# Attention over one core: PSUM banks of the score ring and the logit ring shared out as four and two in place of three and three

## The reference

```python
xn = _ln(x, norm_s_w, norm_s_b)
spatial_out = _spatial_experts(xn, idx_s, sp_in_w, sp_in_b, sp_out_w, sp_out_b)
xt = _ln(x, norm_t_w, norm_t_b)
temporal_out = _temporal_experts(xt, idx_t, tq_w, tq_b, tk_w, tk_b, tv_w, tv_b, tp_w, tp_b)
fused = _cross_mha(spatial_out, temporal_out, cross_in_w, cross_in_b, cross_out_w, cross_out_b)
x = x + fused
h2 = _ln(x, norm_mlp_w, norm_mlp_b)
x = x + (jax.nn.gelu(h2 @ mlp_w1.T + mlp_b1, approximate=False) @ mlp_w2.T + mlp_b2)
```

## Time and profile before

| What | Value |
|---|---|
| Median of 3 runs | 1720.06 us (1719.16 to 1722.15) |
| Profiled execution | 1724.92 us |
| its span, first to last instruction | 1723.1 us |
| mean granted clock of TensorE | 0.937 |
| TensorE busy | 1531.3 us (89%) |
| VectorE busy | 1244.2 us (72%) |
| ScalarE busy | 1103.0 us (64%) |
| GpSimd busy | 1021.3 us (59%) |

### The profile page before, as it was taken

The page is one execution under the profiler, slowest core; times in us unless marked ns, Lnnn a source line. Parts: engine busy times, 40 slices in busy tenths (PEclk is TensorE's granted clock), DMA queues, the critical chain, the costliest instruction groups (busy, mean ns, idle before and its releaser), DMA issues. The chain is left out here.

```text
span 1723.1 us, 37357 instructions
## 1 busy us (share of the span) xinstructions
PE 1531.3 (89%) x8662; PEld 660.2 (38%) x8662; DVE 1244.2 (72%) x3454; ACT 1103.0 (64%) x2137; POOL 1021.3 (59%) x1375
## 2 busy tenths in 40 slices
PE   2767965889999999999999999999999999875998
PEld 0215962233333333333333333333333333212665
DVE  4995865578787878878787887878788787453442
ACT  1433760647877777787877778777777778824333
POOL 6841434366685676667576667658667675432443
PEclk9767976889999999999999999999999999957999
DMA  1321116355464565465465456446546544030221
GB/s 40 77 54 30 45 30 101 50 78 73 72 81 63 71 76 77 59 80 75 59 79 76 70 64 83 64 62 86 66 70 74 82 55 63 2 37 26 62 67 55
DMA packets 134645, 109.27 MB, mean 63 GB/s; under 512 B 24128, under 2 KB 127552, under 8 KB 134592
## 3 DMA queue, kind: packets, MB, share of 16 engines
q1 hardware_dynamic: 132544, 104.45, 41.1%
q0 software_dynamic: 2048, 4.20, 1.0%
HBM read 19.26 MB, written 8.39 MB: 16 GB/s over the span
## 5 line engine op out<-in xcount | busy, mean ns | idle before, releaser
L1124 ACT ACTIVATE probs<-psum 128x512 f32<-128x512 f32 (+3 forms) x1536 | 750.0, 549 | 276.3 <-PE psum L1232 269.1
L1020 DVE TENSOR_REDUCE mx_S<-psum 128x1 f32<-128x512 f32 x512 | 324.7, 679 | 54.1 <-PE psum L1212 54.1
L1020 DVE TENSOR_REDUCE mx_C<-psum 128x1 f32<-128x512 f32 x512 | 317.6, 676 | 35.7 <-PE psum L1212 35.7
L1016 DVE CUSTOM_DVE_ANT_0 psum<-psum,causal 128x128 f32<-128x128 f32 (+3 forms) x512 | 241.4, 516 | 101.5 <-PE psum L1212 100.3
L1212 PE MATMUL psum<-ks_C,qs_C 96*128 96x512 bf16 x512 | 199.8, 398 | 12.1 <-DVE mx_C L1020 9.4
L1212 PE MATMUL psum<-ks_S,qs_S 96*128 96x512 bf16 x512 | 196.9, 395 | 13.3 <-DVE mx_S L1020 9.4
L1232 PE MATMUL psum<-qs_S,ks_S 99*128 99x512 bf16 x512 | 189.0, 385 | 5.4 <-ACT probs L1124 5.4
L1232 PE MATMUL psum<-qs_C,ks_C 99*128 99x512 bf16 x512 | 188.9, 387 | 4.7 <-ACT probs L1124 4.4
L903 POOL CAST parts_q<-f_q 128x512 bf16<-128x512 f32 x48 | 29.3, 611 | 261.8 <-ACT f_q L1115 261.4
L1212 PE MATMUL psum<-ks_T,qs_T 96*128 96x128 bf16 (+3 forms) x512 | 156.7, 308 | 6.4 <-DVE mx_T L1016 4.3
L1232 PE MATMUL psum<-qs_T,ks_T 99*128 99x256 bf16 (+3 forms) x512 | 152.7, 302 | 6.2 <-ACT probs L1124 3.3
(11 more groups left out here) (182 smaller groups left out, 2722.2 us busy)
## 6 DMA issues: line engine op xcount, KB each, us to landing
qs_S<-parts_q SPq DMA_DIRECT2D x96, 128.0 KB, 4.4
ks_S<-parts_k SPq DMA_DIRECT2D x96, 128.0 KB, 5.0
qs_T<-parts_q SPq DMA_DIRECT2D x96, 128.0 KB, 4.4
ks_T<-parts_k SPq DMA_DIRECT2D x96, 128.0 KB, 4.6
qs_C<-parts_q SPq DMA_DIRECT2D x96, 128.0 KB, 4.4
ks_C<-parts_k SPq DMA_DIRECT2D x96, 128.0 KB, 4.7
w_in_S<-in_s_in SPq DMA_DIRECT2D x16, 257.0 KB, 2.7
w_in_T<-in_t_in SPq DMA_DIRECT2D x16, 257.0 KB, 2.6
```

The costliest lines, as they stand in the source:

```text
L1016: nc.vector.tensor_tensor_reduce(tile[:, 0:last_key], tile[:, 0:last_key], causal[:, T - last_key:T], 1.0, NEG, ALU.add, ALU.max, mx[kind] ...
L1020: nc.vector.tensor_reduce(mx[kind][:, n:n + 1], tile, AX_X, ALU.max, negate=True).then_inc(reduced, 1)
L1124: nc.scalar.activation(probs[:, group_place(kind, b, n // 4), n % 4, t0:T], psum[:, LOGITS + ring_place(kind, b, n, RC), t0:T], ACT.Exp, s ...
```

## The change

The score ring gets a fourth bank and the logit ring gives one up. The bank of the weighted sums (6) and the desk (7) stay where they are. Score tile n then waits for the reduction of tile n-4 in place of n-3, and logit tile n for the exponential of tile n-2 in place of n-3. The logit ring begins at bank 4 in place of 3; the fold of weights ahead of the loop, which borrows the first two logit banks, moves with it.

```diff
-RL, RC, RP = 3, 3, 3
+RL, RC, RP = 4, 2, 3
```

## The result

The changed kernel takes 1826.05 us (median of 4, 1821.69 to 1827.05) against 1720.05 (median of 4 on the same chip): 1.0612 of the time before, 95% interval 1.0599 to 1.0625. The forecast was 1810 (1738 to 1840), slower.

A forecast was written before the change was run, and what follows sets the result against it. TensorE's own work and short stalls were taken to set the loop's period; 7.1 lost less 1.1 kept gives 6.0 us a cycle, times 15 cycles 90 us, so 1810 us (1738 to 1840).

The forecast's parts named there:

- What bounds the kernel: Attention loop, cycle 76.2 us: TensorE's own work and its short stalls set the period; no other engine is full.
- Part 2, the third logit bank: Attention loop: logit tiles wait for exponential n-2, not n-3, making 24 groups late by 7.1 us a cycle together.
- Part 1, the fourth score bank: Attention loop: score tiles stall 3.2 us a cycle on reductions; one more bank keeps 1.1 us of that as gain.
- the four stalls counted as kept: Score stalls where logits have room: S tile 9 0.49, T tile 9 0.36, C tile 9 0.15, T tile 29 0.07.
- The 0.78 us that stood at 796.15: Largest score stall, 0.78 us; not kept, since the logits at 796.38 then wait for an exponential behind the reciprocal.
- The sum: Whole kernel: 15 cycles x 6.0 us = 90 us more, leaving out the first logit unit and the last two.
- B: Loop: longer period takes back groups late only through ScalarE's other work, 4.8 us a cycle; 18 us slower, 1738; chance 0.20.
- C: Loop: VectorE holds the cycle and a score tile ahead pays in full, 51 us faster, 1669; chance 0.08.
- E: Whole kernel: gains and losses cancel within 3 us, about 0.2%; chance 0.04.
- D: Loop: more stalls bring the clock from 1.00 to 0.87, 249 us more, 1969; chance 0.06.

The follow-up runs named there:

- the kernel with three and two banks: Against the kernel before, only the third logit bank taken away, score ring kept at three banks: 1829.28 us, 1.0640.
- half exponentials and the reciprocal moved: Against the kernel before: four score and two logit banks, exponentials over half their columns, reciprocal at step 26 instead of 23; 1712.85 us, one execution.
- three and three with half exponentials: The kernel before, three score and three logit banks, with each exponential covering only the first half of its columns: 1699.12 us, one execution.

## Why the prediction held, point by point

**What bounds the kernel.** Shown for the loop: less its logit and score stalls by starts, the cycle is 71.8 to 71.9 us in each of the eight kernels with whole exponentials (cycles of 76.2 to 84.5) and 71.4 to 71.7 in the three with half ones. From kernel to kernel VectorE's and ScalarE's busy time in a cycle differs by less than 2 us wherever the same exponentials run.

**Part 2, the third logit bank: 7.1 us a cycle.** The direction and the mechanism are shown by the kernel with three and two banks. That kernel loses 6.40 us, net of the score stalls that the late logits absorb. In the changed kernel, read from the start of one weighted sum to the next, 22 of the 24 groups (each net of its recovered score stall) came within 0.03 us of the forecast; the group of S's first logits came out 0.10 better, that of T's logits 22 to 25 0.12 better.

**Part 1, the fourth score bank: 1.1 us kept of 3.2.** Too large by half: on top of the late logits it is worth 0.55 us. Of the four stalls counted as kept, only that of S tile 9 is the bank's: 0.46 is still there with three and two banks and gone with four and two. Those of T tile 9, C tile 9 and T tile 29 (0.58 in all) are gone with three score banks too, since each stands right behind a logit tile that is late by the prediction's own list (S's first 0.36, T's first 0.20, S's sixth group 0.36), which gives the reductions time. The net is not touched by this, as such a stall ends with either share; 7.1 and 1.1 were both too high by that 0.58, and the net 6.0 came close to 5.85 for that reason. The 0.78 us that stood at 796.15 came back as a wait for ScalarE, as said; in the changed kernel this is the tile at 823.80.

```profile
822.95 0.63 ACT L1139 ACTIVATE s_recip<-s_right 128x512 f32<-128x512 f32 x1 [0.75 <-DVE s_right L1057]
823.49 1.34 ACT L1124 ACTIVATE probs<-psum 128x128 f32<-128x128 f32 x3
823.80 0.39 PE L1232 MATMUL psum<-qs_T,ks_T 99*128 99x512 bf16 x1 [0.94 <-ACT probs L1124]
```

**The sum: 15 x 6.0 = 90 us.** The medians differ by 106.0 us, so 16 of them were missed. The rate was right (5.85 to 5.87); the count of cycles was not. The term that was mis-sized is what lies outside the 13 loop cycles: I gave it two cycles, 12 us, on the ground that TensorE has holes there to hide the loss. Measured from the first score tile on: 3.8 us ahead of the loop (134.6 to 138.4), 5.7 over the next two units, 11.3 over the late stretch and 5.1 from there to the end, 25.9 in all. With three and two banks the late stretch alone lost 5.9 us, so a ring of two costs more there and not less: 3.2 us over the 32 C logit tiles that run alone, where the eight C groups of that kernel's steady cycle lose 2.5. The rest of the late stretch came with the clock. Why the ring costs more where no score tiles run beside the logits was not tried. 76.3 + 25.9 = 102.2 us; the profiled executions differ by less, 96.7 in span, since the one of the changed kernel reached the first score tile 5.7 us earlier (279.38 for 285.05). That is the spread of executions and not the change: the other two kernels with three and three banks and whole exponentials reach it at 279.06 and 280.42.

**The rivals.** B (the longer period takes back what stands behind ScalarE's other work) did not come true: those groups lost what the reading said, and the reciprocal alone was worth 2.03 us a cycle when moved. C (faster) fell with the result and with the share of three and two, by which the fourth score bank is worth 0.55 us and not 3.2; E (no change) fell with the result. Even with half exponentials and the reciprocal moved, four and two banks (75.71) did not overtake three and three with half exponentials (75.27). D (the clock) was wrong for the loop, 1.00 throughout with 9.9 us of stalls a cycle, and came true in one place that I had not looked at, the late stretch, for some 5 us; the sum had no term for that.

## What to carry to other kernels

When two rings share the same banks, read for each ring how late a tile would start behind the reader one bank earlier, group by group; that gave the loop's new period to 0.15 us, while the sums of waits pointed to the wrong ring. A stall right behind a tile that will be late is not the other ring's to give back. A spare bank hides the odd work that a reader does between two tiles, so before taking one away, count that work, and see whether it can stand where the reader is idle anyway. Count the drain of a pipeline apart from its loop: the balance of engines is another there.

## What was not expected of the hardware

The steady loop kept a clock of 1.00 with 37 waits of up to 1.3 us in a cycle of 82 us. In the late stretch, where logits and weighted sums run alone, the clock read 0.78 over 1564 to 1603 in the changed kernel, and 1.00 with 40 extra matmuls in the same window. Over the same 32 logit tiles it read 1.00 with three and two banks (24.0 us) and 0.71 with four and two (29.4 us), though both kernels came to them at the same 29.30 us of the stretch.
